# A decoder layer in one kernel: a reordered mixing cycle, and batch 0 of the output projection moved into the end of attention

## The reference, cut to what matters

```python
# 1. mixing ("attn"), per batch; cumsum runs over the tokens
pos_values = x @ Wpv + bpv
pos_ret = (pos_cos * cumsum(pos_cos * pos_values) + pos_sin * cumsum(pos_sin * pos_values)) / sqrtD
key_ph = tanh(x @ Wk + bk) * pi;  kv_values = x @ Wkv + bkv
value_gates = sigmoid(gelu([x, shift1(x)] @ Wg1 + bg1) @ Wg2 + bg2)
kv_ret = (cos(key_ph) * cumsum(...) + sin(key_ph) * cumsum(...)) / (sqrt(gate_cumsum) * sqrtD)
bw = softmax(gelu(x @ Wb1 + bb1) @ Wb2 + bb2)
blended = bw[..., 0:1] * pos_ret + bw[..., 1:2] * kv_ret
x = layernorm(x + x + layernorm_affine(blended) @ Wo + bo)
# 2. cross attention, 16 heads of 16 features, 1601 keys; softmax over the queries (axis 1)
x = layernorm(x + attn(x, ctx) @ Wo + bo)
# 3. 8 experts, the best two of each token, weighted by a softmax over the two
x = layernorm(x + sum_e w_e * (relu(x @ W1[e] + b1[e]) @ W2[e] + b2[e]))
```

## Time and profile before

| | us |
|---|---|
| median of 3 timed runs (lowest 2199.92, highest 2205.04) | 2202.6 |
| the profiled execution's own time | 2195.98 |
| its span | 2194.3 |
| PE busy | 1981.7 (90%) |
| DVE (VectorE) busy | 1754.2 (80%) |
| ACT (ScalarE) busy | 1540.5 (70%) |
| POOL (GpSimd) busy | 736.3 (34%) |

### The profile page before, as it was taken

The page is one execution under the profiler, slowest core; times in us unless marked ns, Lnnn a source line. Parts: engine busy times, 40 slices in busy tenths (PEclk is TensorE's granted clock), DMA queues, the critical chain, the costliest instruction groups (busy, mean ns, idle before and its releaser), DMA issues.

```text
span 2194.3 us, 43516 instructions
## 1 busy us (share of the span) xinstructions
PE 1981.7 (90%) x10630; PEld 1044.8 (48%) x10638; DVE 1754.2 (80%) x3559; ACT 1540.5 (70%) x4345; POOL 736.3 (34%) x983
## 2 busy tenths in 40 slices
PE   7898998899999999999999998888829999999994
PEld 3554555322322232222322221112729999999994
DVE  5889885799999999999999999998635555555554
ACT  4655565899999999999999999998402333233333
POOL 0112111244444444444444441111563333333333
PEclk9989999999999999999999999999859999999997
DMA  4111105776758576676668576661771222222225
GB/s 156 44 44 72 58 24 130 193 125 116 112 110 145 118 110 117 119 124 135 90 131 136 108 111 92 123 77 42 223 197 32 37 36 37 36 36 36 36 36 168
DMA packets 126117, 212.39 MB, mean 97 GB/s; under 512 B 31554, under 2 KB 94786, under 8 KB 124882
## 3 DMA queue, kind: packets, MB, share of 16 engines
q1 hardware_dynamic: 98272, 151.74, 37.8%
q0 software_dynamic: 26240, 59.00, 10.2%
q10 hardware_dynamic: 1554, 1.05, 0.2%
HBM read 138.38 MB, written 73.74 MB: 97 GB/s over the span
## 4 chain that ended last, share of the span: by engine, by line
PE 39%; ACT 30%; issue 18%; DVE 7%; POOL 3%; DMA 2%; ACTq 1%; DVEq 0%; SPq 0%; POOLq 0%
ACT w_all L1429 26%; PE psum L1715 12%; PE psum L1725 11%; PE psum L473 6%; DVE neg_max L1336 3%; POOL list_all L1595 3%; PE psum L1239 2%; PE psum L1271 2%; ACT w_all L822 1%; PE psum L1702 1%; DMA v_all<-w_all 1%; PE psum L500 1%; ACTq L1428 1%; DVE stats L1016 0%; DVE stats L1995 0%
## 5 line engine op out<-in xcount | busy, mean ns | idle before, releaser
L1429 ACT ACTIVATE w_all<-psum,neg_max 128x512 f32<-128x512 f32 (+1 forms) x1664 | 1111.1, 736 | 18.2 <-DVE neg_max L1336 16.6
L1336 DVE TENSOR_REDUCE neg_max<-psum 128x1 f32<-128x512 f32 (+1 forms) x1664 | 1024.9, 677 | 17.3 <-PE psum L1271 14.2
L1271 PE MATMUL psum<-qst,kst 96*128 96x512 bf16 (+1 forms) x1664 | 527.7, 389 | 73.1 <-ACT w_all L1429 63.1
L1239 PE MATMUL psum<-w_all 128*32 128x512 f32 (+1 forms) x3328 | 448.9, 612 | 9.5 <-DVE w_all L1350 9.3
L1271 PEld LDWEIGHTS psum<-qst,kst 96*128 96x128 bf16 (+1 forms) x1664 | 130.0, 98 | 658.1 <-ACT w_all L1429 639.0
L1769 ACT ACTIVATE hid<-psum,b 128x128 f32<-128x128 f32 x568 | 161.9, 368 | 393.1 <-PE psum L1715 393.1
L1429 ACT ACTIVATION_READ_ACCUMULATOR w_all<-psum,neg_max 128x1 f32 (+1 forms) x1664 | 426.8, 257 | 0.0
L1402 POOL TENSOR_TENSOR w_all<-vst,inv 128x64 f32<-128x64 f32 (+1 forms) x416 | 121.0, 291 | 658.3 <-DVE inv L1304 654.7
L1715 PE MATMUL psum<-xst,w 128*128 128x128 f32 x2272 | 267.4, 277 | 0.0
L1715 PEld LDWEIGHTS psum<-xst,w 128*128 128x128 f32 x2272 | 261.6, 193 | 0.1
L1725 PE MATMUL psum<-area,hid 128*128 128x256 f32 x1136 | 257.0, 380 | 0.0
(11 more groups left out here) (209 smaller groups left out, 1878.1 us busy)
## 6 DMA issues: line engine op xcount, KB each, us to landing
kst<-k_parts SPq DMA_DIRECT2D x384, 112.0 KB, 6.5
k_parts<-k_out POOLq DMA_DIRECT2D x52, 336.0 KB, 3.0
w_all<-in_W SPq DMA_DIRECT2D x16, 1024.0 KB, 11.9
area<-in_ctxT SPq DMA_DIRECT2D x16, 896.0 KB, 4.7
vst<-v_all SPq DMA_DIRECT2D x64, 224.0 KB, 9.2
qst<-q_parts SPq DMA_DIRECT2D x192, 64.0 KB, 5.9
v_all<-area POOLq DMA_DIRECT2D x13, 896.0 KB, 4.3
q_parts<-q_out POOLq DMA_DIRECT2D x24, 256.0 KB, 3.0
```

The source lines that it names most:

```text
L1239: last = pe.matmul(psum[j * PAD:(j + 1) * PAD, 6, :], v_scaled[0:r, pb, j, :], probs_at[pb][0:r, j, :], start=t == 0, stop=t == ST - 1)
L1271: pe.matmul(psum[0:r, 2 * sbuf + i, :], kst[:, h, j, t * P:t * P + r], qst[:, h, j, :], start=True, stop=True).then_inc(scores_ready, 1)
L1336: v.tensor_reduce(neg_max[0:r, sbuf, i:i + 1], psum[0:r, 2 * sbuf + i], AX_X, ALU.min) \
L1429: act.activation(probs_at[pb][0:r, j, :], psum[0:r, 2 * sbuf + i, :], ACT.Exp, bias=neg_max[0:r, sbuf, i:i + 1], scale=-1.0, accum_out=sum ...
```

## The change

In the mixing step, PE's `mix_out` and the means are split by token tiles and interleaved, and the mean squares come between the two chunks of the value projection. VectorE does both scans of `mem_s` and the product `mem_c * pos_cos` ahead of the variance. In the last round of attention, PE projects batch 0 between two `pv` groups, and VectorE norms it ahead of the last copy out of attention. The routing steps 2 to 7 become a loop with the batch in a register, and `ranks` no longer waits for `slots_ready`. Before the first expert tile, VectorE copies b1 and W1 ahead of the row numbers, and W1 and W2 have a semaphore each. The final `out_ready` shares a semaphore with `x1_ready`.

```diff
-                def mix_out(e):
-                    pe.wait_ge(blended_ready, e + 1)
-                    for t in range(TT):
+                def mix_out(e, ts):
+                    for t in ts:
...
-                    last.then_inc(mix_out_ready, 1)
+                    if ts[-1] == TT - 1:
+                        last.then_inc(mix_out_ready, 1)
...
-                        mix_out(e)
+                        pe.wait_ge(blended_ready, e + 1)
+                        mix_out(e, (0, 1))
                         if not drain:
                             pe.wait_ge(bw_z_read, c + 1)
-                        mix_stats(e)
+                        mix_means(e, (0, 1))
+                        mix_out(e, (2, 3))
+                        mix_means(e, (2, 3))
                     if not drain:
                         if not end:
                             pe.wait_ge(gate_h_ready, c + 1)
-                        project(2, wkv, now(h), C).then_inc(kv_ready, 1)
+                        project(2, wkv, now(h), C, range(1))
+                    if end:
+                        mix_squares(e)
+                    if not drain:
+                        project(2, wkv, now(h), C, range(1, C)).then_inc(kv_ready, 1)
...
                         v.wait_ge(pv_used, c + 1)
-                        s_s = scan(mem_s, 0)
+                        for i in range(C):
+                            s_s = scan(mem_s, i)
+                        v.wait_ge(dve_front, s_c)
+                        times(mem_c, mem_c, pos_cos)
...
                         v.tensor_tensor(var_c[:], var_c[:], psum[:, 7, TT:2 * TT], ALU.add).then_inc(var_ready, 1)
-                    if mix:
-                        s_s = scan(mem_s, 1)
-                    if end:
...
                         v.wait_ge(dve_front, s_s)
-                        times(mem_c, mem_c, pos_cos)
                         s = times(mem_s, mem_s, pos_sin)
...
+                    if tile == N_TILE + 1 and is_over(tile, it):
+                        pe.wait_ge(xwo_loaded, 16)
+                        pe.wait_ge(exp_done, 2 * N_SUB * it + 2 * LAST_OF_FIRST + 2 + 2 * CREDIT)
+                        project_rows(pe, 0, 0, 1, range(TT))
                     if tile >= LAG:
                         pv(tile - LAG, it)
...
+                    if tile == N_TILE + LAG - 1 and is_over(tile, it):
+                        v.wait_ge(v_scaled_ready, N_TILE * (it + 1))
+                        norm_rows(v, 0, 0)
                     for h in range(2):
                         if tile == ST * (h + 1) + LAG - 1:
...
+            def route_steps(eng, step, turns, last):
...
+                for c in range(2):
+                    one(c, 0, c, c)
+                with eng.Fori(1, turns) as it:
+                    for h in range(2):
+                        one(2 * it + h, it, h, 2 + h)
+                for c in range(2 * turns, last):
+                    one(c, c // 2, c % 2, c)
...
                     pe.wait_ge(mask_ready, s + 1)
-                    wait(pe, slots_ready, s)
...
                 opened(pe, mm1_done, mm2_done)
-                pe.wait_ge(xwo_loaded, 16)
-                project(0, range(TT))
-                for c in range(B + 2):
-                    route_step(c)
+                route_steps(pe, route_step, B // 2 - 1, B + 2)
...
                 v.sem_inc(y_scaled, 1)
-                for d in range(3):
-                    name_rows(d, 16)
-                v.wait_ge(ffn_loaded, 32 * E)
-                at = copy_weights(slice(0, 1), 0)
-                v.wait_ge(xs_t_ready, 1)
-                take_rows(0)
-                v.wait_ge(b2_loaded, 16)
-                scale_bias(at, 0)
+                v.wait_ge(w1_loaded, 16 * E)
                 v.wait_ge(x2_ready, B)
                 for h in range(2):
                     v.wait_ge(x2_stored[h], 16 * B)
+                at = copy_first(slice(0, 1), 0)
+                for d in range(3):
+                    name_rows(d, 16)
+                v.wait_ge(xs_t_ready, 1)
+                take_rows(0)
+                v.wait_ge(w2_loaded, 16 * E)
+                copy_second(at, 0)
+                v.wait_ge(b2_loaded, 16)
+                scale_bias(at, 0)
                 tiles(v, tile_step)
```

More of the change, by code:

```diff
@@ L1135, in decoder_layer @@
             CREDIT = N_TILE
+            LAST_OF_FIRST = max(k for k in range(N_SUB) if score_buf[k] == 0)
             def free(k, buffer_of, it):
@@ L1540, in decoder_layer, with wide, project_rows @@
             assert TILES % DESTS == 3 and TT * D == HID and B >= 4
+            def wide(t):
+                return t.rearrange("p t d -> p (t d)").rearrange("p (n f) -> p n f", n=2)
+            def project_rows(pe, b, h, loads, ts):
+                if ts[0] == 0:
+                    wait(pe, y2_ready, b - 1)
+                    pe.wait_ge(route_loaded[h], 32 * loads)
+                for t in ts:
+                    at = psum[:, 2 * h + t // 2, (t % 2) * D:(t % 2 + 1) * D]
+                    for k in range(C):
+                        last = pe.matmul(at, at_in[:, h, k, t * P:(t + 1) * P], xwo[:, k, :], start=k == 0,
+                                         stop=k == C - 1)
+                if ts[-1] == TT - 1:
+                    last.then_inc(proj_ready, 1)
@@ new lines, in norm_rows @@
+            def norm_rows(v, c, h):
+                norms = Steps(NORM_STEPS * c)
+                wait(v, x2_ready, c)
+                v.wait_ge(proj_ready, c + 1)
+                v.tensor_tensor(wide(y2), psum[:, 2 * h:2 * h + 2], wide(x1_in[:, h]), ALU.add) \
+                    .then_inc(y2_ready, 1)
+                v.wait_ge(y2_ready, c + 1)
+                for t in range(TT):
+                    v.bn_stats(stats2[:, t], y2[:, t]).then_inc(dve_norm, 1)
+                    s = norms.next()
+                wait_alone(v, (dve_norm, s))
+                for t in range(TT):
+                    last = v.bn_aggr(moments2[:, t], stats2[:, t])
+                last.then_inc(moments2_ready, 1)
@@ L1562, in tile_step @@
                         load_list(bass.ds(n + 3, 1), (d + 3) % DESTS)
-                for c in range(B):
-                    route_step(c)
+                route_steps(sp, route_step, B // 2 - 1, B)
                 for e in range(W2_EARLY, E):
@@ L1643, in experts_tensor, with turn @@
             def experts_tensor(pe):
[L1644 to L1658 removed]
+                def turn(e, h):
                     wait(pe, x2t_copied, e)
@@ L1772, in experts_scalar @@
                 act.preload_act_table_set("natural_log_exp_and_others")
[L1773 to L1774 removed]
+                route_steps(act, route_step, B // 2, B + 1)
                 tiles(act, tile_step)
```

151 lines of the change are left out of this document (61 added, 90 removed).

## The result

The changed kernel takes **2253.4 us** (median of 5 runs, 2251.1 to 2254.9), the kernel before 2205.0 in the same comparison (5 runs, 2199.9 to 2209.5): a ratio of 1.0233, interval 1.0218 to 1.0247. The forecast was 2218, range 2202 to 2227. The direction was right, the size was not: the profiled executions differ by 2252.1 - 2194.3 = 57.8 us, and 16.2 were expected.

A forecast was written before the change was run, and what follows sets the result against it. No engine bounds the whole; the mixing loop runs over PE, ACT and a short DVE chain. Terms 10.2 + 1.1 + 6.0 - 1.1 = +16.2 us on 2196.0 give 2212.2; with 6.6 for timed runs 2218.8, stated as 2218, range 2202 to 2227.

The forecast's parts named there:

- Part 4: Loops, semaphores, first tile: loop instructions hidden, W1 copied earlier gains 1.1 us, tile loop and attention unchanged.
- Part 1: Mixing order on PE: longer idle gap before turn drops the clock, four short periods become long, +10.2 us.
- Part 2: Mixing order on VectorE: y starts 0.5 us earlier, against squares 0.65 us later, over 7 steps, +1.1 us.
- Part 3: Batch 0 in attention: late copy delays load of batch 2 by 3.5 us, half clock follows, first scatter later, +6.0 us.
- First tile: First expert tile: copying W1 ahead of the row numbers takes xst off PE's path, -1.1 us (0 to -2.2).
- The first: Rival, mixing on PE: the clock survives the gap, +1.0 us in all, 2203.6 us; chance 0.10.
- the second: Rival, routing: the load of batch 2 does not delay the scatters, +8.3 us in all, 2211 us; chance 0.13.
- the third: Rival, mixing: VectorE's chain bounds the step, so the change is faster, 2187 or 2196 us; chance 0.13.

The follow-up runs named there:

- e1: Kernel before plus two instructions (already met waits) in VectorE's program ahead of the attention loops; 2228.7 us in its one timed run.
- e2: Changed kernel with two instructions fewer in VectorE's mixing loop, so its attention loop stands where it stood before; 2225.5 us, ratio 1.0109.
- e11: e2 plus four filling matmuls in PE's idle time ahead of turn in the mixing steps; profiled span 2209.3 us.
- e7: e2 with the squares ahead of the whole value projection again, mix_out and means still interleaved; profiled span 2205.3 us.
- e8: e2 with PE's mixing order as before and VectorE's as changed; profiled span 2194.6 us.
- e9: Kernel before with VectorE's half of the mixing change alone, its attention loop where it was; 2194.6 us, ratio 0.9960.
- e12: e8 with the copy out of attention ahead of the norm of batch 0 in attention's last turn; profiled span 2196.8 us.
- e14: e8 with the load of batch 2 put ahead of the wait for the last copy out of attention in SP's queue; 2198.7 us, ratio 0.9988.
- e5: Changed kernel plus 64 instructions (met waits) in VectorE's program ahead of the attention loops; 2227.7 us in its one timed run.

## Why the prediction was wrong, point by point

- **Part 4, "the tile loop and attention are unchanged"** is the step that failed: this term was put at 0, without a row for it, and measured +34.0 us. The instructions of the loop were unchanged, their place was not, and e1 and e2 show that two instructions ahead decide. The profile of before has no row that prices this; it has one fetch in the loop, and I did not read the code queue at all. That VectorE is late for want of its code is inferred from the fetches at each pause; that the place of the loop decides is shown. With that term the sum would have been 16.2 + 34.
- **Part 1**, +10.2: confirmed in size. Measured were 11.9 us for the whole stage against 11.3 with part 2, periods of 43.8 to 44.4 against 43.5 to 44.5, idle time 5.16 against 4.9, turn 1.94 against 1.9. The mechanism (gap, half clock) is shown by e11. Of the full matmuls that I saw coming between one-column ones, only the half projection ahead of the squares makes the steps long. Those between the means are in e7 too, whose steady steps take 40.9 us.
- **Part 2**, +1.1: the net of two terms that cannot be seen apart in the changed kernel. VectorE's order by itself gives 5.9 to 7.7 us (e8, e9), not 3.5: I priced y's earlier start, and not that with the shorter gap (1.1 us) the clock falls at fewer turns.
- **Part 3**, +6.0: right in its chain, too small. Copy 4.6 us later against the last exponential (forecast 4.7), load of batch 2 3.3 us later (3.5), half clock in projection and route (3.75 and 3.42 us). Two terms were mis-sized. The first is what lies between: from the issue to PE's start 8.3 us, where I carried over the 5.75 of before. That was not the load's time: PE stood behind `turn` then, and the second part of the load (L191) landed 4.8 us after its issue; in e2 it took 7.7. x2's stores and the load of batch 3 now follow at once and may share the DMA engines with it; in e12 the load of batch 3 comes 4.3 us behind, not 1.9, and it still took 7.3. Which of them slows it was not separated. The second is the half clock, from PE's start to the first scatter 17.2 us against 12.1, so +5.1 where I had 2.5: it reached further, through the second half projection and the next turn (from the logits to the first scatter 10.2 us, against 8.5 before).
- **First tile**, -1.1: 9.1 us from list load to the first mm1 before, 7.6 after, so -1.5. That it was eaten in the profile (+1.3 from first scatter to mm1) lies in the wait for the list, 9.6 us against 7.3. Over the sixteen profiles this wait is 5.5 to 13.0 us and follows none of the edits. What sets it stays open.
- The **rivals**: none had the loop's code. The first did not come: behind each of the six full gaps turn took 1.94 us. Nor the second: PE waited 7.77 us for the load of batch 2. Nor the third, VectorE's chain: it needed shorter periods, and they were 43.8 to 44.4 us.

The range was too narrow because it was made of the terms I had, and all of them were edits that I had looked at.

## What to carry to other kernels

An edit changes the place of all code behind it. When a loop's time moves that nobody touched, compare the code queue's packets inside the loop before looking for a cause in data or semaphores, and try one or two instructions more or fewer ahead of it. For TensorE, ask of each order not only how long the matmuls take but how long the gap is that they leave on the loop: the same work may be cheaper when it ends later. And a step pulled ahead on one engine gains nothing here while the loads that it frees stand behind another engine's late work in the same queue; with one load moved out (e14), the next one took its place.

## What the runs showed that was not expected

- Two instructions that do nothing, in VectorE's program, cost 2.7 us in each of twelve turns of a loop of 291 instructions (e1: 73.2 against 70.5), in which five 8 KB fetches run per turn; 64 more ahead of it, and it is gone (e5).
- The profile names as releaser of VectorE's 2.45 us the semaphore of PE, which had been done 0.7 us before the end of the wait. A wait at a branch with fetches of code beside it looks like a wait for data.
- TensorE's granted clock is 0.62 in the mean over nine microseconds in which it was never idle (e8), with one-column matmuls at their start. Why it falls there is open.
